# Four-head graph attention: the sum over edges and the own loop joined by TensorE's accumulation instead of a VectorE addition

## What is computed

```
x = (meta_x @ W).reshape(N, HEADS, DIM)
logits = leaky_relu(a_src[src] + a_dst[dst])
ex = exp(logits - segment_max(logits, dst)[dst])
alpha = ex / segment_sum(ex, dst)[dst]
out = segment_sum(x[src] * alpha, dst)
return out.mean(axis=1) + bias
```

## Time and profile before

| | |
|---|---|
| Median of three runs | 7980.62 us (7980.48 to 7987.24) |
| The profiled execution | 7990.91 us, of which the span is 7989.2 us |
| VectorE busy over the span | 5563.0 us (70%) |
| GpSimd busy | 5200.0 us (65%) |
| TensorE busy, its weight loads | 2985.7 us (37%), 2378.1 us (30%) |
| ScalarE busy | 2917.5 us (37%) |

### The profile page before, as it was taken

One profiled execution on the slowest core, in us unless ns is written; L12 is line 12 of the kernel. 1 busy time (PEld: TensorE's weight loads), 2 busy tenths in 40 slices (PEclk: granted clock), 3 DMA queues, 4 the chain that ended last, 5 costly groups with the idle time before them and its releaser, 6 DMA issues. The chain is left out here.

```text
span 7989.2 us, 77514 instructions
## 1 busy us (share of the span) xinstructions
PE 2985.7 (37%) x14049; PEld 2378.1 (30%) x14049; DVE 5563.0 (70%) x16528; ACT 2917.5 (37%) x6586; POOL 5200.0 (65%) x5145
## 2 busy tenths in 40 slices
PE   4776700211111116777756634454400000362322
PEld 1222200211111116666646634444300000252221
DVE  6667687877767757777879969999634444463764
ACT  3555523433333334444434436666500000121211
POOL 0003774777777767777666547777567777777677
PEclk9888855555555557888856655555555555675555
DMA  8884217111111115555579944444321111663321
GB/s 103 112 115 98 69 18 64 27 26 25 25 25 25 25 35 154 169 176 178 167 254 308 311 139 146 147 154 147 125 56 45 45 45 44 141 225 108 97 92 61
DMA packets 786583, 864.06 MB, mean 108 GB/s; under 512 B 469875, under 2 KB 483427, under 8 KB 779804
## 3 DMA queue, kind: packets, MB, share of 16 engines
q1 hardware_dynamic: 572556, 684.47, 30.1%
q0 software_dynamic: 163408, 175.42, 10.5%
q10 hardware_dynamic: 50240, 0.60, 0.6%
HBM read 419.15 MB, written 480.23 MB: 113 GB/s over the span
## 5 line engine op out<-in xcount | busy, mean ns | idle before, releaser
L164 POOL DMA_INDIRECT T<-slot_at,home_row x393 | 433.5, 1103 | 814.9 <-DVE home_row L728 676.1
L1244 POOL DMA_INDIRECT e_other<-X,index x392 | 426.4, 1088 | 179.2 <-issue 117.8
L1232 POOL DMA_INDIRECT e_ahead<-XA,index x392 | 417.4, 1065 | 178.8 <-issue 118.9
L3032 POOL DMA_INDIRECT e_got<-G,index x392 | 370.2, 944 | 244.1 <-issue 112.3
L1892 POOL DMA_INDIRECT e_mine<-T,index x392 | 394.6, 1007 | 203.0 <-issue 114.3
L3661 POOL DMA_INDIRECT out_rows<-e4s_out,index x392 | 419.0, 1069 | 165.3 <-issue 118.8
L2383 PE MATMUL e_turned<-ident,e_own_x 128*128 128x128 f32 x196 | 54.6, 434 | 1233.9 <-DVE e_own_x L1971 1233.9
L1904 POOL DMA_INDIRECT X<-e_row,index x392 | 421.4, 1075 | 125.3 <-issue 118.8
L3470 POOL DMA_INDIRECT rows<-X,index x392 | 398.1, 1015 | 129.9 <-issue 129.9
L1255 POOL DMA_INDIRECT XA<-e4d_sent,index x392 | 393.2, 1003 | 119.4 <-issue 118.8
L1244 POOL DMA_INDIRECT e4d_other<-X,index x392 | 375.0, 957 | 136.1 <-issue 118.2
(11 more groups left out here) (695 smaller groups left out, 13110.3 us busy)
## 6 DMA issues: line engine op xcount, KB each, us to landing
XA<-e_n_xa SPq DMA_DIRECT2D x49, 1056.0 KB, 5.2
SUMS<-e_state SPq DMA_DIRECT2D x49, 1056.0 KB
e4n_n_xa<-XA SPq DMA_DIRECT2D x49, 1056.0 KB, 5.3
X<-e_n_row SPq DMA_DIRECT2D x49, 576.0 KB
X<-pl_x SPq DMA_DIRECT2D x98, 268.0 KB, 2.2
e_n_x<-X SPq DMA_DIRECT2D x49, 536.0 KB
B<-e_n_b SPq DMA_DIRECT2D x49, 528.0 KB
e_n_b<-B SPq DMA_DIRECT2D x49, 528.0 KB, 6.7
```

What stands on the lines that cost most here:

```text
L164: gp.indirect_dma_start(out=words, out_offset=bass.IndirectOffsetOnAxis(ap=home_row[:, t:t + 1], axis=0), in_=slot_at[:, t:t + 1], in_offs ...
L1232: gp.indirect_dma_start(out=ahead[:, b, j, :], out_offset=None, in_=g.XA[0:SLOTS, :], in_offset=bass.IndirectOffsetOnAxis(ap=index_of(g, 0 ...
L1244: gp.indirect_dma_start(out=other[:, h, j, :], out_offset=None, in_=others[:, :], in_offset=bass.IndirectOffsetOnAxis(ap=index_of(g, s, 1, ...
```

## The change

The addition `joined` is taken out, with the step "z" of its semaphore. TensorE's `turn` makes two products with the identity instead of each transpose, one of `z[:, 0]` and one of `z[:, 1]`, and accumulates them in the same place of PSUM. Its wait for "z" becomes two, for `scaled` ("z0") and for the own-loop products (`loop_made`). `loop_products` gets a wait until the previous chunk has been turned, since `z[:, 1]` is now read by TensorE. SyncE's load of the own rows waits for the own-loop products and for "qadd" of the slot's previous chunk instead of "z". The factor beta is put into PSUM; alpha stays in SBUF under a name of its own.

```diff
-            share = sb("share", [P, 2, J, H])
+            alpha = sb("alpha", [P, J, H])
...
-            z_turned = ps("z_turned", [P, 2 * J, P])
+            z_turned, beta = ps("z_turned", [P, 2 * J, P]), ps("beta", [P, J, H])
...
-            end_dve = Engine(sem(f"{name}_end_dve"), "most f1 f2 g1 g2 g3 beta al0 alpha z0 z")
+            end_dve = Engine(sem(f"{name}_end_dve"), "most f1 f2 g1 g2 g3 beta al0 alpha z0")
...
                             if begun(c[0], RING):
-                                sp.wait_ge(end_dve.sem, end_dve.after(n - RING, "z"))
+                                sp.wait_ge(loop_made.sem, loop_made.after(n - RING))
+                                sp.nop(nofuse=True)
+                                sp.wait_ge(loops.sem, loops.after(n - RING, "qadd"))
                                 sp.nop(nofuse=True)
...
-                    if end and kind == "heads":
-                        joined(end, J)
...
-                    end_dve.done(v.tensor_tensor(share[:, 0, :, :], fin[:, 0, :, :], most[:, 3, :, :], ALU.mult), "beta")
+                    end_dve.done(v.tensor_tensor(beta[:, :, :], fin[:, 0, :, :], most[:, 3, :, :], ALU.mult), "beta")
...
                         last = v.tensor_tensor(z[:, 0, 0:count, part], state[:, h, 0:count, part],
-                                               share[:, 0, 0:count, q].unsqueeze(2).to_broadcast([P, count, D]), ALU.mult)
+                                               beta[:, 0:count, q].unsqueeze(2).to_broadcast([P, count, D]), ALU.mult)
...
-                def joined(c, count):
-                    n = c.n
-                    v.wait_ge(end_dve.sem, end_dve.after(n, "z0"))
-                    v.wait_ge(loop_made.sem, loop_made.after(n))
-                    for q in range(H):
-                        part = slice(q * D, (q + 1) * D)
-                        last = v.tensor_tensor(z[:, 0, 0:count, part], z[:, 0, 0:count, part], z[:, 1, 0:count, part], ALU.add)
-                    end_dve.done(last, "z")
...
                     a.wait_ge(end_dve.sem, end_dve.after(n, "alpha"))
+                    if begun(c, 1):
+                        a.wait_ge(end_pe.sem, end_pe.after(n - 1, "z3"))
...
-                    t.wait_ge(end_dve.sem, end_dve.after(n, "z"))
+                    t.wait_ge(end_dve.sem, end_dve.after(n, "z0"))
+                    t.wait_ge(loop_made.sem, loop_made.after(n))
...
-                            last = t.transpose(z_turned[:, 4 * i + r, :], z[:, 0, j, q * P:(q + 1) * P], g.ident[:, :])
+                            t.matmul(z_turned[:, 4 * i + r, :], lhsT=z[:, 0, j, q * P:(q + 1) * P], rhs=g.ident[:, :], start=True, stop=False)
+                            last = t.matmul(z_turned[:, 4 * i + r, :], lhsT=z[:, 1, j, q * P:(q + 1) * P], rhs=g.ident[:, :], start=False, stop=True)
```

More of the change, by code:

```diff
@@ L1559, in shares @@
                     need("g3")
-                    end_dve.done(v.tensor_tensor(share[:, 0, :, :], fin[:, 0, :, :], most[:, 3, :, :], ALU.mult), "beta")
+                    end_dve.done(v.tensor_tensor(beta[:, :, :], fin[:, 0, :, :], most[:, 3, :, :], ALU.mult), "beta")
                     end_dve.done(v.tensor_tensor(most[:, 4, :, :], fin[:, 1, :, :], most[:, 3, :, :], ALU.mult), "al0")
                     need("al0")
-                    end_dve.done(v.tensor_scalar(share[:, 1, :, :], most[:, 4, :, :], -1.0, None, ALU.add), "alpha")
+                    end_dve.done(v.tensor_scalar(alpha[:, :, :], most[:, 4, :, :], -1.0, None, ALU.add), "alpha")
                 def scaled(c, count):
@@ L1635, in _ @@
                     c = FIX
-                    v.wait_ge(end_dve.sem, end_dve.after(NCH - 1, "z"))
+                    v.wait_ge(end_dve.sem, end_dve.after(NCH - 1, "z0"))
+                    v.wait_ge(loop_made.sem, loop_made.after(NCH - 1))
                     v.tensor_copy(mine[:, c.slot, 0, :], g.fix_x2[:, :]).then_inc(set_up, 1)
@@ L1645, in _ @@
                     scaled(c, 1)
-                    joined(c, 1)
                     y_rows(c, 1, g.fix_b2[:, :].unsqueeze(1))
@@ L1700, in loop_products @@
                     a.wait_ge(end_dve.sem, end_dve.after(n, "alpha"))
+                    if begun(c, 1):
+                        a.wait_ge(end_pe.sem, end_pe.after(n - 1, "z3"))
                     for j in range(count):
                         for q in range(H):
-                            last = a.activation(z[:, 1, j, q * D:(q + 1) * D], mine[:, h, j, 8:], ACT.Copy, scale=share[:, 1, j, q:q + 1])
+                            last = a.activation(z[:, 1, j, q * D:(q + 1) * D], mine[:, h, j, 8:], ACT.Copy, scale=alpha[:, j, q:q + 1])
                     loop_made.done(last)
```

## The result

The changed kernel takes 7874.86 us (median; 7870.33 to 7880.12), the kernel before 7983.35 us beside it: a ratio of 0.9864, 95% interval 0.9847 to 0.9881. The forecast was 7878. The median gain is 108.5 us.

What follows compares the result with a forecast made beforehand. VectorE (DVE) was taken to bound the four-head stage; 110.9 - 5 - 3 = 103 us off it gave 7878 us against the median of 7981, with an 8-in-10 range of 7860 to 7948.

Steps and rivals of the forecast that it cites:

- The addition: L1586 on VectorE in the four-head stage goes: 2.41 us a round, 46 rounds, at most 110.9 us gained.
- DVE's round: VectorE's own period in the four-head stage, from one L1576 to the next, falls from 20.65 to 18.24 us.
- The turning: TensorE's 16 transpose records become 64 product records: 9.3 us a round (8.8 to 10.2) against 3.37.
- The new loop: Turning (L), ScalarE's last copy, own-loop products and handoffs: a round of at least L + 8.65; cost 5 us in all.
- The rival on the other side: The loop through TensorE and ScalarE binds at the low clock, if it never rises about 8100 us; chance 0.12.
- POOL let go: Without the stall over L1586, GpSimd's 14 gathers per chunk need 18.1 us instead of 19.6.
- I take DVE's value: Of VectorE's 18.24 us a round and GpSimd's 18.1, 0.1 apart, the forecast uses VectorE's as the bound.
- the second rival: GpSimd binds because its stall stays or moves to another VectorE instruction: 19.6 us a round, about 7932; chance 0.09.
- The share factor: VectorE's scaling (L1576) by a factor in PSUM: -6 to +9 us over 46 rounds, taken as nothing.
- the 12 us estimated from the errata section: 62 more cycles per PSUM-source instruction: four scalings cost 0.26 us a round, making the gain 12 us smaller.
- The moved waits and the fixed-up row: Changed waits of SP, ScalarE and TensorE cost nothing; the final row's some 6 us more turning is covered by 30 us.
- The tail: In the last chunks nothing covers the longer turning: 3 us lost together.

Runs made afterwards that it cites:

- idle_add: The changed kernel with four VectorE additions of 128x512 f32 put back at the old place, into a spare tile nobody reads: 7983.19 us, ratio 0.9995.
- turn96: The changed kernel with each first product of the turning issued twice, 96 TensorE records a round instead of 64: 8027.40 us, ratio 1.0046.
- early: The changed kernel with TensorE's 16 products of the scaled sums first, then the own loop's 16, which alone wait for ScalarE: 7870.82 us, ratio 0.9844.
- idle_scale: The changed kernel with four unread VectorE multiplications by the share factor, broadcast from PSUM, at the old addition's place: 7978.05 us, ratio 0.9984.
- factor_sbuf: The changed kernel with the share factor beta put back into SBUF, nothing else different: 7878.09 us, ratio 0.9864.
- before_products: The kernel before with its 16 transposes written as 16 full f32 products with the identity, addition kept: 7990.86 us, ratio 0.9997.

## Why the prediction was right, step by step

- **The addition.** Right. 2.41 us a round were foreseen; 2.43 less were measured over 48 rounds, and idle_add puts 2.39 back (20.47 against 18.08). I had counted 46 rounds; of the other two the first was paid in full (2.64 us) and the last in part (0.92), a third of what the sum lacked.
- **DVE's round.** 18.24 foreseen, 18.08 found. idle_add has a round of 20.47 where the kernel before has 20.63, so the other parts of the edit give 0.16. Taken from the start of each instruction to the start of the next, it lies in the running sums (0.06), the copy in front of them (0.06), L1411 (0.04) and L1576 (0.02). What makes these shorter stays open.
- **The turning.** Right: 9.3 us (8.8 to 10.2) foreseen, 9.47 in the mean (8.75 to 10.36) of the 33 turnings that start from 4900 to 5500 us, with the clock rising on the way. The middle of 3.3 and 6.1 is 4.7 and not 4.4; with it the same sum gives 9.5.
- **The new loop.** L + 8.65 foreseen, L + 8.5 in turn96. Its cost was put at 5 us; L1576 waited 2.8 us for PE, and early, whose loop is shorter, took 3.0 off the whole stage. The rival on the other side named the right mechanism: turn96 makes a turning of 13 us and is slower than the kernel before. By these numbers it cancels the gain at a turning of about 12.1 (20.63 less 8.5), above the longest one of 10.4.
- **POOL let go.** Right in its price, 18.1 foreseen and 18.06 found, and in its cause: the long gathers come with the additions (idle_add) and not with any VectorE work in their place (idle_scale), and the longest one in the middle of the changed kernel's stage takes 1.47 us. "I take DVE's value" was too narrow: the two stand level. idle_scale shows that GpSimd's relief alone gives little. Without it the round would have stayed at 19.6 by the sum, as the second rival had it; no run relieves VectorE alone in the kernel before, so that is argued and not shown.
- **The share factor.** Nothing foreseen. For VectorE that holds (682 ns against 689); the 12 us estimated from the errata section of the Trainium skill's page "VectorE: DVE Perf Modes" did not show. The prediction did not see the effect on GpSimd's gathers, 1.07 us instead of 0.95 over L1576.
- **The moved waits and the fixed-up row.** Right. SP waits 657.6 us instead of 791.2 for its new releaser; VectorE's last instruction of the stage stands at 5689.38, GpSimd's last gather at 5714.09.
- **The tail.** -3 foreseen, -2.7 found.

Against the forecast of 103 us the stage gave 113.8. The two rounds make 3.6 of the 11; the other 46 gave 7 more than forecast, 0.15 a round, since the loop cost less than the 0.11 put down for it and the other parts of the edit gave something. That the median lies only 3 us from the forecast is in part luck: the stage gave 11 us more than the sum, while the medians of the whole kernels differ by 108.5.

## What to carry to other kernels

Where two engines are within a few per cent of each other, read both rounds, and ask of a change whether it relieves both. The addition had cost VectorE 2.4 us and GpSimd 1.5 us a round (19.57 to 18.06 for 14 gathers), and only because it went from both could the round come down to 18.1: by the sums GpSimd alone would have held it at 19.6, and with GpSimd alone relieved it stayed at 20.4 (idle_scale). Before moving work onto an idle engine, write down the loop that it closes: here turning + 8.5 us, good up to a turning of 12 and a loss beyond, as turn96 with 12.9 showed.

## What the runs showed of the hardware

A gather issued by GpSimd took 0.94 to 0.97 us beside a VectorE scaling with its factor in PSUM (L1576 of the changed kernel), 1.07 in the mean and 1.44 at most with that broadcast factor in SBUF (factor_sbuf), and 2.2 to 3.2 where it was held up by the four additions of two whole SBUF tiles (idle_add). I had not expected the place of a factor of 32 values per partition to matter to another engine.

This is no price of every instruction with two inputs in SBUF. The running sums read two and left the gathers at 0.94 to 1.07 us. In an earlier stage of the kernel before, a single addition of two whole SBUF tiles of 128x512 (L2015) left the 17 gathers that lie over it for more than half a microsecond at 0.94 to 0.98. How many such instructions follow each other, here four in 2.5 us, and where in them a gather starts was not varied.

In before_products the granted clock was 0.50 from the start of the 32 products to 5224.1 us and 1.00 behind that, so the weights' products right behind them ran at 2.4 GHz (3.79 us). After the 16 transposes of the kernel before the clock rose as well: it was 0.50 from 5216.5 to 5219.4, 1.00 from 5219.5 to 5222.8 and 0.50 from 5222.9 to 5229.6. But TensorE then waited 2.81 us for ScalarE's copies and began the weights' products at 5222.67, so these ran at 1.2 GHz nearly throughout (6.98 us). Since TensorE bounded neither kernel, the faster products were worth nothing: 0.9997.
